# Four-layer graph network on one core: the variance and the negated mean of node phases 0 and 3 move from VectorE to GpSimd, and the gate of phase 3 becomes one product

## The chip, the cores and the metric

The kernel runs on one core of a Trainium2 chip. The metric is the device time of one execution in microseconds; 6471.27 us is the median of three runs of the kernel before.

## The reference

Four graph layers run one after the other on 50,000 nodes of 160 values (64 scalars, 32 vectors of three) and 25,000 edges. Each computes messages on the edges, adds them up by node, and ends with a residual and a normalisation:

```python
x = _layernorm(x + _L0_gnn_ref(x, ...), axis=-1)      # and so for L1, L2, L3
# _layernorm: (x - mean(x)) / sqrt(var(x) + 1e-5), over the 160 values of a node
# L0, node part:
angle = 0.1 * (ms @ W3) * node_attr * (1.0 / np.sqrt(MUL0 + MUL1))
cos, sin = (jnp.cos(angle), jnp.sin(angle))
return cos * sc + sin * conv                          # sc: a product of x with weights
# L3, node part: out_s, out_v = the sums from the edges plus a product of x with weights
fs = jax.nn.silu(out_s[:, :MUL0])
gate = jax.nn.sigmoid(out_s[:, MUL0:MUL0 + 32])
gv = gate[:, :, None] * out_v
return jnp.concatenate([fs, gv.reshape(N, -1)], axis=-1)
```

## The kernel before

Each layer has an edge phase, which adds messages into a table `agg` in device memory, and a node phase, which reads `x` and `agg` and writes the new `x`. The change touches two node phases: that of layer 0 (`node_phase_01`, called node phase 0) and that of layer 3 (`node_phase_3`).

A node phase goes over the nodes in 98 chunks of 512: 128 partitions with T = 4 nodes on each. Every engine has its own list of stages with a lag, `node_pipeline(engine, ((lag, stage), ...))`. At step m it runs its stages in the order of that list, each for chunk m - lag. The first 16 chunks and the last ones are written out, and the middle is a loop of eight chunks per turn. Engines meet by semaphores only; work buffers are double (`u = r % 2`), those of the transfers eightfold. GpSimd follows each wait with `fence`, an increment of a semaphore of its own. In the names of the trace the phase's tag is left out of this text: `rs` is `rs_n` there.

Node phase 0. SP loads `xr` and `ar`. TensorE transposes `xr` (L614, L617); ScalarE copies that to SBUF (`xta` L638, `xtb` L640); TensorE multiplies by the weights into `pk` (L625, L626). GpSimd makes the angle from `ar` (stage `angles`, `th` L720, `rn` L723, `th` L726 and L729), ScalarE its sine and cosine (stage `sines`, `ab` L646, `sn` L647, `cs` L649), and GpSimd the two factors (stage `factors`, `at` L737, `cf` L738). VectorE forms `y` = `pk` * `at` + `xr` (L680), then `ar` * `cf` + `y` (L686), the statistics of each node (`st` L693) and their mean and variance (`mv` L700), and in the stage `variance` `ve` = variance + 1e-5 (L706) and `nm` = -mean (L707). GpSimd's stage `deviation` raises `ve` to the power -1/2 (`rs` L751) and multiplies `nr` = `nm` * `rs` (L754). ScalarE's stage `normalise` writes `xn` = `rs` * `y` + `nr` (L657), which SP stores. The order of stages on an engine is

```python
node_pipeline(a, ((0, copy_turned), (4, normalise)) + (((1, sines),) if l == 0 else ()))
node_pipeline(v, ((3, skips), (3, sums), (3, moments), (3, join), (3, variance)))
node_pipeline(pool, ((1, factors), (3, deviation), (1, attribute)) + (((0, angles),) if l == 0 else ()))
```

Node phase 3 begins in the same way. VectorE's stage `layer` forms the scalars `ss` (L2154) and vectors `sv` (L2155) from `ar` and `pk`. ScalarE's stage `gates` makes `gt` = tanh(s/2) (L2130), and silu of the other scalars into `sg` (L2131). VectorE's stage `gate` multiplies (`gt` + 1) with `sv` into `sg`, one instruction for each of the four tiles (L2163); `total` adds `xr` into `y` (L2171); `moments` and `variance` make `st` (L2178), `mv` (L2186), `ve` (L2189) and `nm` (L2190). GpSimd has `deviation` alone (`rs` L2202, `nr` L2205); ScalarE's `normalise` is L2139. The order is

```python
node_pipeline(a, ((0, copy_turned), (3, normalise), (1, gates)))
node_pipeline(v, ((1, layer), (2, gate), (2, total), (2, moments), (2, variance)))
```

Of the kernel before, what the change touches and what calls it, by code (L numbers as in the profile page):

```python
# [23 lines left out]
P = 128  # L24
# [6 lines left out]
T = 4  # L31
# [494 lines left out]
def node_phase_01(nc, l, x, agg, xo, wt, width):  # L526

    with ExitStack() as ctx:
# [18 lines left out]
        cf = each(2, sb, "cf", [P, T])  # L547
        y = each(2, sb, "y", [P, T, D])
        st = sb("st", [P, T, 6])
        mv = sb("mv", [P, T, 2])  # L550
        ve = each(2, sb, "ve", [P, T])
        nm = each(2, sb, "nm", [P, T])
        rs = each(2, sb, "rs", [P, T])
        nr = each(2, sb, "nr", [P, T])
        xn = each(RN, sb, "xn", [P, T, XW])
# [107 lines left out]
        @block.vector  # L663
        def _(v):
            v.tensor_scalar(wt(f"na_{l}")[0:S0], wt(f"na_{l}")[0:S0], 1.0 / 8.0, None, ALU.mult).then_inc(folded, 1)
            v.tensor_scalar(wt(f"na_{l}")[S0:P], wt(f"na_{l}")[S0:P], 32.0 ** -0.5, None, ALU.mult).then_inc(folded, 1)
            v.tensor_scalar(wt(f"nb_{l}"), wt(f"nb_{l}"), 32.0 ** -0.5, None, ALU.mult).then_inc(folded, 1)
            if l == 0:
                v.memset(quarter[:], np.pi / 2).then_inc(folded, 1)
                v.tensor_scalar(turns[:], wt("attr"), 0.1 * 10.0 ** -0.5 * 96.0 ** -0.5 / (2 * np.pi), None, ALU.mult).then_inc(folded, 1)  # L670
                v.tensor_scalar(share[:], wt("attr"), 960.0 ** -0.5, None, ALU.mult).then_inc(folded, 1)

            def skips(c, r, k, parts):
                u = r % 2
                v.wait_ge(k_ps, c + 1)
                v.wait_ge(cf_ok, NCF * (c + 1))
                v.wait_ge(xn_ok, due(T * (c - 1)))
                for t in range(T):
                    by = at[u][:, t:t + 1] if l == 0 else xr[r][:, t, D:XW]
                    v.scalar_tensor_tensor(y[u][:, t, :], pk[u][:, t, 0:D], by, xr[r][:, t, 0:D], ALU.mult, ALU.add).then_inc(sk_ok, 1)  # L680

            def sums(c, r, k, parts):
                u = r % 2
                for t in range(T):
                    v.wait_ge(sk_ok, T * c + t + 1)
                    v.scalar_tensor_tensor(y[u][:, t, :], ar[r][:, t, 0:D], cf[u][:, t:t + 1], y[u][:, t, :], ALU.mult, ALU.add).then_inc(y_ok, 1)  # L686

            def moments(c, r, k, parts):
                u = r % 2
                v.wait_ge(st_ok, 8 * c)  # L690
                for t in range(T):
                    v.wait_ge(y_ok, T * c + t + 1)
                    v.bn_stats(st[:, t, :], y[u][:, t, :]).then_inc(st_ok, 1)  # L693

            def join(c, r, k, parts):
                v.wait_ge(ve_ok, 2 * c)
                v.wait_ge(st_ok, 8 * c + 4)
                fence(v)
                for t in range(T):
                    v.bn_aggr(mv[:, t, :], st[:, t, :]).then_inc(st_ok, 1)  # L700

            def variance(c, r, k, parts):
                u = r % 2
                v.wait_ge(st_ok, 8 * c + 8)
                v.wait_ge(rs_ok, due(2 * (c - 1)))
                v.tensor_scalar(ve[u][:], mv[:, :, 1], EPS, None, ALU.add).then_inc(ve_ok, 1)  # L706
                v.tensor_scalar(nm[u][:], mv[:, :, 0], -1.0, None, ALU.mult).then_inc(ve_ok, 1)  # L707

            node_pipeline(v, ((3, skips), (3, sums), (3, moments), (3, join), (3, variance)))

        @block.gpsimd
        def _(pool):
# [32 lines left out]
            def deviation(c, r, k, parts):  # L745
                u = r % 2
                pool.wait_ge(xn_ok, due(T * (c - 1)))
                fence(pool)
                pool.wait_ge(ve_ok, 2 * c + 2)
                fence(pool)  # L750
                pool.tensor_tensor(rs[u][:], ve[u][:], wt("mhalf"), ALU.pow).then_inc(rs_ok, 1)  # L751
                pool.wait_ge(rs_ok, 2 * c + 1)
                fence(pool)
                pool.tensor_tensor(nr[u][:], nm[u][:], rs[u][:], ALU.mult).then_inc(rs_ok, 1)  # L754

            pool.wait_ge(folded, 6)
            node_pipeline(pool, ((1, factors), (3, deviation), (1, attribute)) + (((0, angles),) if l == 0 else ()))
# [1268 lines left out]
def node_phase_3(nc, x, agg, out, wt):  # L2026

    with ExitStack() as ctx:  # L2028
# [8 lines left out]
        ss = each(2, sb, "ss", [P, T, 96])  # L2037
        sv = each(2, sb, "sv", [P, T, V3])
        gt = each(2, sb, "gt", [P, T, V1])
        sg = each(2, sb, "sg", [P, T, D])  # L2040
        y = each(2, sb, "y", [P, T, D])
        st = sb("st", [P, T, 6])
        mv = sb("mv", [P, T, 2])
        ve = each(2, sb, "ve", [P, T])
        nm = each(2, sb, "nm", [P, T])
        rs = each(2, sb, "rs", [P, T])
        nr = each(2, sb, "nr", [P, T])
        xn = each(RN, sb, "xn", [P, T, D])
# [66 lines left out]

        @block.scalar
        def _(a):
# [8 lines left out]
            def gates(c, r, k, parts):  # L2126
# [2 lines left out]
                a.wait_ge(y_ok, due(c - 1))  # L2129
                a.activation(gt[u][:], ss[u][:, :, S0:96], ACT.Tanh, scale=0.5).then_inc(act_ok, 1)  # L2130
                a.activation(sg[u][:, :, 0:S0], ss[u][:, :, 0:S0], ACT.Silu).then_inc(act_ok, 1)  # L2131

            def normalise(c, r, k, parts):

# [3 lines left out]
                for t in range(T):  # L2138
                    a.activation(xn[r][:, t, :], y[u][:, t, :], ACT.Identity, bias=nr[u][:, t:t + 1], scale=rs[u][:, t:t + 1]).then_inc(xn_ok, 1)  # L2139

            node_pipeline(a, ((0, copy_turned), (3, normalise), (1, gates)))

        @block.vector
        def _(v):
            v.tensor_scalar(wt("na_3")[:, 96:192], wt("na_3")[:, 96:192], 0.5, None, ALU.mult).then_inc(folded, 1)
            v.tensor_scalar(wt("nb_3"), wt("nb_3"), 0.5, None, ALU.mult).then_inc(folded, 1)

            def layer(c, r, k, parts):
# [30 lines left out]

            def variance(c, r, k, parts):  # L2180
                u = r % 2
                v.wait_ge(ve_ok, 2 * c)
                v.wait_ge(st_ok, 8 * c + 4)
                fence(v)
                for t in range(T):
                    v.bn_aggr(mv[:, t, :], st[:, t, :]).then_inc(st_ok, 1)  # L2186
                v.wait_ge(st_ok, 8 * c + 8)
                v.wait_ge(rs_ok, due(2 * (c - 1)))
                v.tensor_scalar(ve[u][:], mv[:, :, 1], EPS, None, ALU.add).then_inc(ve_ok, 1)  # L2189
                v.tensor_scalar(nm[u][:], mv[:, :, 0], -1.0, None, ALU.mult).then_inc(ve_ok, 1)  # L2190
# [4 lines left out]
        def _(pool):  # L2195
            def deviation(c, r, k, parts):
                u = r % 2
                pool.wait_ge(xn_ok, due(T * (c - 1)))
                fence(pool)
                pool.wait_ge(ve_ok, 2 * c + 2)  # L2200
                fence(pool)
                pool.tensor_tensor(rs[u][:], ve[u][:], wt("mhalf"), ALU.pow).then_inc(rs_ok, 1)  # L2202
                pool.wait_ge(rs_ok, 2 * c + 1)
                fence(pool)
                pool.tensor_tensor(nr[u][:], nm[u][:], rs[u][:], ALU.mult).then_inc(rs_ok, 1)  # L2205

            node_pipeline(pool, ((2, deviation),))

# [598 lines left out]
```

## Time and profile before

| | before |
|---|---|
| median of three runs | 6471.27 us (6468.07 to 6472.73) |
| the profiled execution | 6468.58 us |
| its span, first to last instruction | 6466.8 us |
| busy over the span: TensorE | 5101.9 us (79%) |
| VectorE | 4234.2 us (65%) |
| ScalarE | 2848.6 us (44%) |
| GpSimd | 4361.7 us (67%) |
| node phase 0, `rs` of the first to `rs` of the last chunk | 910.4 to 1338.3 us |
| node phase 3, the same | 6012.1 to 6460.2 us |

The shares are means over stages of very different kinds: edge phases fill most of the span. For the two node phases the timeline and the waits of their own stretch have to be read.

### The profile page before, as it was taken

How to read it: one execution, taken by the hardware profiler on the slowest of the kernel's cores; microseconds unless marked ns; L12 is line 12 of the kernel's file. 1: busy time of each engine (PE TensorE's matmuls, PEld its weight loads, DVE VectorE, ACT ScalarE, POOL GpSimd, SP SyncE). 2: the span in 40 equal slices, each digit the busy share in tenths (PEclk: the TensorE clock that was granted, in tenths of full speed). 3: DMA queues.
4: the chain of work that ended last, by engine and by line, in shares of the span. 5: the costliest groups of instructions: out<-in, count | busy, mean ns of one | idle time of the engine just before them, and what ended most of it. 6: DMA issues, size and time to landing. Idle time of an engine off the chain costs nothing. (4 is left out here: it accounts for less than half of the span.)

```text
span 6466.8 us, 123966 instructions
## 1 busy us (share of the span) xinstructions
PE 5101.9 (79%) x27989; PEld 3926.1 (61%) x28012; DVE 4234.2 (65%) x14730; ACT 2848.6 (44%) x6258; POOL 4361.7 (67%) x4641
## 2 busy tenths in 40 slices
PE   8889966679997886999655434338999989998776
PEld 6556656646666885767422134337888867776665
DVE  3566658854544786888677621216888878776788
ACT  5333347744443554444200000006777764443666
POOL 8688856658886877766277678875666657887222
PEclk9899989979998998999888766668999999999999
DMA  8566667736665663555311244443333325554665
GB/s 323 124 121 122 124 161 223 221 103 127 130 129 158 206 206 122 162 163 159 130 34 32 61 97 76 74 56 99 107 108 109 109 88 92 85 87 66 225 224 186
DMA packets 584565, 845.56 MB, mean 131 GB/s; under 512 B 216827, under 2 KB 334035, under 8 KB 579859
## 3 DMA queue, kind: packets, MB, share of 16 engines
q1 hardware_dynamic: 405587, 691.27, 33.5%
q0 software_dynamic: 178752, 151.88, 16.7%
q8 instruction: 68, 1.11, 0.1%
q14 instruction: 158, 1.29, 0.1%
HBM read 465.84 MB, written 375.78 MB: 130 GB/s over the span
## 5 line engine op out<-in xcount | busy, mean ns | idle before, releaser
L1143 POOL DMA_INDIRECT xg<-x,gidx x588 | 608.2, 1034 | 244.4 <-issue 181.1
L330 POOL DMA_INDIRECT agg<-summed,cidx x392 | 630.4, 1608 | 196.0 <-issue 111.5
L2020 PE MATMUL pc_a<-msg_a,same_a 128*128 128x168 f32 x980 | 258.1, 450 | 403.3 <-ACT summed_a L2007 346.4
L2020 PEld LDWEIGHTS pc_a<-msg_a,same_a 128*128 128x128 f32 x980 | 245.0, 305 | 416.9 <-issue 290.2
L403 DVE TENSOR_TENSOR pr<-pf,ws 128x512 f32<-128x512 f32 x196 | 135.6, 692 | 512.7 <-PE pf L490 395.6
L1154 POOL DMA_INDIRECT agg<-summed,cidx x196 | 317.5, 1620 | 78.2 <-issue 57.3
L1966 POOL DMA_INDIRECT agg<-summed_a,cidx_a x196 | 311.5, 1589 | 69.6 <-issue 58.5
L1317 ACT ACTIVATE ob<-po 128x416 f32<-128x416 f32 (+1 forms) x392 | 197.7, 504 | 354.0 <-PE po L1394 185.0
L1886 PE MATMUL pm_m<-arow_m,ones_m 128*128 128x512 bf16 x392 | 151.5, 477 | 227.6 <-DVE top_m L1833 225.3
L519 PEld LDWEIGHTS pc<-ob,same 128*128 128x128 f32 x1960 | 279.5, 194 | 83.4 <-issue 83.4
L2202 POOL TENSOR_TENSOR rs_n<-ve_n,wsb 128x4 f32<-128x4 f32 x98 | 98.7, 1007 | 338.0 <-DVE nm_n L2190 338.0
L2109 PE MATMUL pk_n<-wsb,xta_n 128*128 128x192 f32 x784 | 214.7, 356 | 121.2 <-ACT xtb_n L2124 121.2
L519 PE MATMUL pc<-ob,same 128*128 128x161 f32 x1960 | 303.4, 311 | 6.5 <-ACT summed L457 6.5
L1380 PE MATMUL ph<-esT,wsb 128*128 128x512 f32 x588 | 302.1, 595 | 2.3 <-DMA trow<-in_src_r 2.3
L625 PE MATMUL pk_n<-wsb,xta_n 128*128 128x160 f32 x784 | 190.2, 324 | 125.4 <-DVE y_n L680 112.6
L2007 ACT ACTIVATE summed_a<-pc_a 128x672 f32<-128x672 f32 x49 | 35.8, 731 | 561.1 <-DMA agg<-summed_a,cidx_a 559.0
L1252 DVE TENSOR_TENSOR pr<-pf,ws 128x512 f32<-128x512 f32 (+1 forms) x245 | 168.4, 687 | 150.8 <-PE pf L1368 83.9
L497 PE MATMUL ph<-hs,wsb 64*128 64x512 f32 x392 | 229.2, 666 | 47.9 <-ACT ws L444 45.5
L2556 POOL TENSOR_TENSOR rsa_n<-var_n,wsb 128x8 f32<-128x8 f32 x98 | 160.4, 1637 | 155.0 <-DVE var_n L2489 155.0
L1956 POOL DMA_INDIRECT big_a<-mx,tidx_a x196 | 197.1, 1006 | 92.0 <-issue 46.9
L1833 DVE TENSOR_REDUCE top_m<-pm_m 128x8 f32<-128x1024 f32 x196 | 238.7, 1221 | 24.6 <-PE pm_m L1888 24.1
L1303 ACT ACTIVATE ws<-ph 128x512 f32<-128x512 f32 x294 | 176.8, 601 | 171.2 <-PE ph L1380 166.9
(354 smaller groups left out, 17650.5 us busy)
## 6 DMA issues: line engine op xcount, KB each, us to landing
ar_n<-agg SPq DMA_DIRECT2D x194, 322.0 KB
agg<-zero SPq DMA_DIRECT2D x50, 768.0 KB
ar_n<-agg SPq DMA_DIRECT2D x97, 384.0 KB
agg<-zero SPq DMA_DIRECT2D x50, 672.0 KB
ar_n<-agg SPq DMA_DIRECT2D x97, 336.0 KB
agg<-zero_h SPq DMA_DIRECT2D x25, 1288.0 KB, 5.4
agg<-zero SPq DMA_DIRECT2D x50, 644.0 KB
x<-xn_n SPq DMA_DIRECT2D x97, 324.0 KB, 3.5
```

Source lines behind the costliest of these rows:

```text
L330: pool.indirect_dma_start(agg, bass.IndirectOffsetOnAxis(ap=cidx[r][:, t:t + 1], axis=0), summed[u][:, t, :], None, compute_op=ALU.add).th ...
L497: pe.matmul(ph[:], wt(f"w{g + 1}_{l}"), hs[NH - 1][:], start=True, stop=True).then_inc(w_ps, 1)
L519: last = pe.matmul(pc[:, t, 0:W], same[u][:, s, t * P:(t + 1) * P], ob[u][:, s, 32:32 + W], start=(s == t), stop=(s == T - 1))
L1143: pool.indirect_dma_start(xg[s][r][:, t, 0:XR], None, x, bass.IndirectOffsetOnAxis(ap=gidx[s][r][:, t:t + 1], axis=0)).then_inc(gathered[r ...
L1154: pool.indirect_dma_start(agg, bass.IndirectOffsetOnAxis(ap=cidx[r][:, t:t + 1], axis=0), summed[u][:, t, :], None, compute_op=ALU.add).th ...
L1317: a.activation(ob[u][:, t, :], po[:, t % 2, 0:TW], ACT.Copy).then_inc(ob_ok, 1)
L1380: pe.matmul(ph[:, (r + g) % 2 if l == 2 else 0], wt(f"w{g + 1}_{l}"), esT[r][:], start=True, stop=True).then_inc(w_ps, 1)
L1833: v.tensor_reduce(top[u][:, t, :], pm[HOME[t]][:], AX.X, ALU.max).then_inc(top_ok, 1)
L1956: pool.indirect_dma_start(big[r][:, t, :], None, mx, bass.IndirectOffsetOnAxis(ap=tidx[r][:, t:t + 1].bitcast(U32), axis=0)).then_inc(big_ ...
L1966: pool.indirect_dma_start(agg, bass.IndirectOffsetOnAxis(ap=cidx[r][:, t:t + 1], axis=0), summed[r % 2][:, t, :], None, compute_op=ALU.add ...
L2020: last = pe.matmul(pc[:, t, 0:W], same[u][:, s, t * P:(t + 1) * P], msg[u][:, s, :], start=(s == t), stop=(s == T - 1))
L2109: pe.matmul(pk[u][:, t, 0:192], xta[u][:, t * P:(t + 1) * P], wt("na_3"), start=True, stop=False)
```

## The change

In both phases `mv` gets two buffers, and `ve` and `nm` have one each. VectorE's chunk ends with `mv`. GpSimd's `deviation` waits for `mv` and for its own last `nr`, and issues `ve`, `nm`, `rs` and `nr`. In phase 3 ScalarE makes `ga` = `gt` + 1 besides (its bias is a column `one` that VectorE sets at the start), and VectorE's gate is one tensor_tensor over the four tiles.

```diff
 node phase 0
             def join(c, r, k, parts):
-                v.wait_ge(ve_ok, 2 * c)
+                v.wait_ge(rs_ok, due(2 * (c - 1)))
                 v.wait_ge(st_ok, 8 * c + 4)
                 fence(v)
                 for t in range(T):
-                    v.bn_aggr(mv[:, t, :], st[:, t, :]).then_inc(st_ok, 1)
-            def variance(c, r, k, parts):
-                u = r % 2
-                v.wait_ge(st_ok, 8 * c + 8)
-                v.wait_ge(rs_ok, due(2 * (c - 1)))
-                v.tensor_scalar(ve[u][:], mv[:, :, 1], EPS, None, ALU.add).then_inc(ve_ok, 1)
-                v.tensor_scalar(nm[u][:], mv[:, :, 0], -1.0, None, ALU.mult).then_inc(ve_ok, 1)
+                    v.bn_aggr(mv[u][:, t, :], st[:, t, :]).then_inc(st_ok, 1)
             def deviation(c, r, k, parts):
                 pool.wait_ge(xn_ok, due(T * (c - 1)))
                 fence(pool)
+                pool.wait_ge(st_ok, 8 * c + 8)
+                fence(pool)
+                pool.wait_ge(rs_ok, 2 * c)
+                fence(pool)
+                pool.tensor_scalar(ve[:], mv[u][:, :, 1], EPS, None, ALU.add).then_inc(ve_ok, 1)
+                pool.tensor_scalar(nm[:], mv[u][:, :, 0], -1.0, None, ALU.mult).then_inc(ve_ok, 1)
                 pool.wait_ge(ve_ok, 2 * c + 2)
                 fence(pool)
-                pool.tensor_tensor(rs[u][:], ve[u][:], wt("mhalf"), ALU.pow).then_inc(rs_ok, 1)
+                pool.tensor_tensor(rs[u][:], ve[:], wt("mhalf"), ALU.pow).then_inc(rs_ok, 1)
 node phase 3: the same, and
@@ scalar
                 a.activation(gt[u][:], ss[u][:, :, S0:96], ACT.Tanh, scale=0.5).then_inc(act_ok, 1)
                 a.activation(sg[u][:, :, 0:S0], ss[u][:, :, 0:S0], ACT.Silu).then_inc(act_ok, 1)
+                a.wait_ge(act_ok, 3 * c + 1)
+                a.activation(ga[u][:], gt[u][:], ACT.Identity, bias=one[:, 0:1], scale=1.0).then_inc(act_ok, 1)
@@ vector
+            v.memset(one[:], 1.0).then_inc(folded, 1)
             def gate(c, r, k, parts):
-                v.wait_ge(act_ok, 2 * c + 2)
+                v.wait_ge(act_ok, 3 * c + 3)
                 v.wait_ge(y_ok, due(c - 1))
-                for t in range(T):
-                    last = v.scalar_tensor_tensor(sg[u][:, t, S0:D].rearrange("p (u c) -> p u c", c=3), gt[u][:, t, :].unsqueeze(2).to_broadcast([P, V1, 3]), 1.0,
-                                                  sv[u][:, t, :].rearrange("p (u c) -> p u c", c=3), ALU.add, ALU.mult)
-                last.then_inc(sg_ok, 1)
+                v.tensor_tensor(sg[u][:, :, S0:D].rearrange("p t (u c) -> p t u c", c=3), sv[u][:].rearrange("p t (u c) -> p t u c", c=3),
+                                ga[u][:].unsqueeze(3).to_broadcast([P, T, V1, 3]), ALU.mult).then_inc(sg_ok, 1)
```

## Rows read from the trace of the kernel before

**Rows 1.** Records of `rs`, phases 0 and 3: count, ns min/median/max, first and last start.
```profile
L751 POOL TENSOR_TENSOR rs_n<-ve_n,wsb x98: 1006/1029/1190, 910.4 to 1338.3; 128x4 f32<-128x4 f32 x98
...
L2202 POOL TENSOR_TENSOR rs_n<-ve_n,wsb x98: 1006/1007/1041, 6012.1 to 6460.2; 128x4 f32<-128x4 f32 x98
```

**Rows 2.** Waits, 950 to 1300 us: us in total, times, longest.
```profile
ACT xn_n L657 <- POOL nr_n L754: 94.8, 79, 1.5
POOL at_n L737 <- ACT cs_n L649: 71.0, 79, 1.0
```

**Rows 3.** Timeline of phase 0: start us, busy us, engine, line, instruction.
```profile
1101.28 0.24 POOL L723 TENSOR_SCALAR rn_n<-th_n 128x4 f32<-128x4 f32 x1 [0.20 <-POOL th_n L720]
...
1101.70 0.20 POOL L726 TENSOR_TENSOR th_n<-th_n,rn_n 128x4 f32<-128x4 f32 x1 [0.18 <-POOL rn_n L723]
...
1102.29 0.16 DVE L707 TENSOR_SCALAR nm_n<-mv_n 128x4 f32<-128x4 f32 x1
...
1103.27 0.20 POOL L737 TENSOR_TENSOR at_n<-cs_n,wsb 128x4 f32<-128x4 f32 x1 [0.94 <-ACT cs_n L649]
1103.42 0.20 POOL L738 TENSOR_TENSOR cf_n<-sn_n,share_n 128x4 f32<-128x4 f32 x1
1103.60 1.03 POOL L751 TENSOR_TENSOR rs_n<-ve_n,wsb 128x4 f32<-128x4 f32 x1
...
1104.81 0.28 POOL L754 TENSOR_TENSOR nr_n<-nm_n,rs_n 128x4 f32<-128x4 f32 x1 [0.18 <-POOL rs_n L751]
...
1105.21 1.76 ACT L657 ACTIVATE xn_n<-y_n,nr_n,rs_n 128x160 f32<-128x160 f32 x4 [0.93 <-POOL nr_n L754]
...
1107.14 0.30 ACT L649 ACTIVATE cs_n<-ab_n,quarter_n 128x4 f32<-128x4 f32 x1
...
1107.71 0.20 POOL L737 TENSOR_TENSOR at_n<-cs_n,wsb 128x4 f32<-128x4 f32 x1 [0.93 <-ACT cs_n L649]
```

**Rows 4.** What ended GpSimd's idle time before `rs`, phase 0: us, times.
```profile
  DVE nm_n L707: 4.7, 2
```

**Rows 5.** Waits, 6050 to 6430 us.
```profile
POOL rs_n L2202 <- DVE nm_n L2190: 265.0, 82, 3.8
```

**Rows 6.** Busy us (x instructions): PE, PEld, DVE, ACT, POOL; clock, DMA share, GB/s.
```profile
6004.00:6008.00 4.00, 4.00 (x33) 4.00 (x32) 1.47 (x3) 1.59 (x4) 0.00 (x0) 0.96 0.85 325
...
6200.00:6250.00 50.00, 36.14 (x264) 33.54 (x263) 44.54 (x180) 34.39 (x87) 13.43 (x22) 1.00 0.66 226
```

**Rows 7.** Timeline of phase 3, one chunk of VectorE and what it depends on.
```profile
6207.32 0.29 ACT L2130 ACTIVATE gt_n<-ss_n 128x128 f32<-128x128 f32 x1
6207.52 0.40 ACT L2131 ACTIVATE sg_n<-ss_n 128x256 f32<-128x256 f32 x1
...
6208.72 0.55 DVE L2154 SCALAR_TENSOR_TENSOR ss_n<-ar_n,pk_n 128x384 f32<-128x384 f32 x1
...
6209.65 0.76 DVE L2163 SCALAR_TENSOR_TENSOR sg_n<-gt_n,sv_n 128x96 f32<-128x96 f32 x4
...
6210.54 0.82 DVE L2171 TENSOR_TENSOR y_n<-sg_n,xr_n 128x640 f32<-128x640 f32 x1
...
6211.01 0.36 PE L2110 MATMUL pk_n<-wsb,xtb_n 128*128 128x96 f32 x2
...
6212.65 0.38 DVE L2186 BATCH_NORM_AGGREGATE mv_n<-st_n 128x2 f32<-128x6 f32 x4 [0.16 <-DVE st_n L2178]
...
6213.06 0.17 DVE L2189 TENSOR_SCALAR ve_n<-mv_n 128x4 f32<-128x4 f32 x1
6213.14 0.16 DVE L2190 TENSOR_SCALAR nm_n<-mv_n 128x4 f32<-128x4 f32 x1
6213.32 0.55 DVE L2154 SCALAR_TENSOR_TENSOR ss_n<-ar_n,pk_n 128x384 f32<-128x384 f32 x1
```

**Rows 8.** Timeline of the edge phase before node phase 3, a product over 384 elements.
```profile
5911.98 0.56 DVE L1270 TENSOR_TENSOR m<-ob,yq 128x384 f32<-128x384 f32 x1
```

**Rows 9.** Records of `nr`, phase 0: ns min/median/max.
```profile
L754 POOL TENSOR_TENSOR nr_n<-nm_n,rs_n x98: 198/280/393, 911.8 to 1339.4; 128x4 f32<-128x4 f32 x98
```

More of the change, by code:

```diff
@@ L549, in node_phase_01 @@
         st = sb("st", [P, T, 6])
-        mv = sb("mv", [P, T, 2])
-        ve = each(2, sb, "ve", [P, T])
-        nm = each(2, sb, "nm", [P, T])
+        mv = each(2, sb, "mv", [P, T, 2])
+        ve = sb("ve", [P, T])
+        nm = sb("nm", [P, T])
         rs = each(2, sb, "rs", [P, T])
@@ L695, in join @@
             def join(c, r, k, parts):
-                v.wait_ge(ve_ok, 2 * c)
+                u = r % 2
+                v.wait_ge(rs_ok, due(2 * (c - 1)))
                 v.wait_ge(st_ok, 8 * c + 4)
@@ L699, in join @@
                 for t in range(T):
-                    v.bn_aggr(mv[:, t, :], st[:, t, :]).then_inc(st_ok, 1)
-            def variance(c, r, k, parts):
-                u = r % 2
-                v.wait_ge(st_ok, 8 * c + 8)
-                v.wait_ge(rs_ok, due(2 * (c - 1)))
-                v.tensor_scalar(ve[u][:], mv[:, :, 1], EPS, None, ALU.add).then_inc(ve_ok, 1)
-                v.tensor_scalar(nm[u][:], mv[:, :, 0], -1.0, None, ALU.mult).then_inc(ve_ok, 1)
-            node_pipeline(v, ((3, skips), (3, sums), (3, moments), (3, join), (3, variance)))
+                    v.bn_aggr(mv[u][:, t, :], st[:, t, :]).then_inc(st_ok, 1)
+            node_pipeline(v, ((3, skips), (3, sums), (3, moments), (3, join)))
         @block.gpsimd
@@ L748, in deviation @@
                 fence(pool)
+                pool.wait_ge(st_ok, 8 * c + 8)
[4 more added lines that the diff above has]
+                pool.tensor_scalar(nm[:], mv[u][:, :, 0], -1.0, None, ALU.mult).then_inc(ve_ok, 1)
                 pool.wait_ge(ve_ok, 2 * c + 2)
                 fence(pool)
-                pool.tensor_tensor(rs[u][:], ve[u][:], wt("mhalf"), ALU.pow).then_inc(rs_ok, 1)
+                pool.tensor_tensor(rs[u][:], ve[:], wt("mhalf"), ALU.pow).then_inc(rs_ok, 1)
                 pool.wait_ge(rs_ok, 2 * c + 1)
                 fence(pool)
-                pool.tensor_tensor(nr[u][:], nm[u][:], rs[u][:], ALU.mult).then_inc(rs_ok, 1)
+                pool.tensor_tensor(nr[u][:], nm[:], rs[u][:], ALU.mult).then_inc(rs_ok, 1)
             pool.wait_ge(folded, 6)
@@ L2039, in node_phase_3 @@
         gt = each(2, sb, "gt", [P, T, V1])
+        ga = each(2, sb, "ga", [P, T, V1])
+        one = sb("one", [P, 1])
         sg = each(2, sb, "sg", [P, T, D])
@@ L2042, in node_phase_3 @@
         st = sb("st", [P, T, 6])
-        mv = sb("mv", [P, T, 2])
-        ve = each(2, sb, "ve", [P, T])
-        nm = each(2, sb, "nm", [P, T])
+        mv = each(2, sb, "mv", [P, T, 2])
+        ve = sb("ve", [P, T])
+        nm = sb("nm", [P, T])
         rs = each(2, sb, "rs", [P, T])
@@ L2111, in skip @@
                 last.then_inc(k_ps, 1)
-            pe.wait_ge(folded, 2)
+            pe.wait_ge(folded, 3)
             node_pipeline(pe, ((0, turn_rows), (1, skip)))
@@ L2139, in normalise @@
                     a.activation(xn[r][:, t, :], y[u][:, t, :], ACT.Identity, bias=nr[u][:, t:t + 1], scale=rs[u][:, t:t + 1]).then_inc(xn_ok, 1)
+            a.wait_ge(folded, 3)
             node_pipeline(a, ((0, copy_turned), (3, normalise), (1, gates)))
@@ L2152, in layer @@
                 v.wait_ge(sg_ok, due(c - 1))
-                v.wait_ge(act_ok, due(2 * (c - 1)))
+                v.wait_ge(act_ok, due(3 * (c - 1)))
                 v.scalar_tensor_tensor(ss[u][:], ar[r][:, :, 0:96], 1.0 / 32.0, pk[u][:, :, 0:96], ALU.mult, ALU.add).then_inc(so_ok, 1)
@@ L2181, in variance @@
                 u = r % 2
-                v.wait_ge(ve_ok, 2 * c)
+                v.wait_ge(rs_ok, due(2 * (c - 1)))
                 v.wait_ge(st_ok, 8 * c + 4)
@@ L2185, in variance @@
                 for t in range(T):
[L2186 to L2190, printed above, removed]
+                    v.bn_aggr(mv[u][:, t, :], st[:, t, :]).then_inc(st_ok, 1)
             node_pipeline(v, ((1, layer), (2, gate), (2, total), (2, moments), (2, variance)))
@@ L2199, in deviation @@
                 fence(pool)
+                pool.wait_ge(st_ok, 8 * c + 8)
+                fence(pool)
+                pool.wait_ge(rs_ok, 2 * c)
+                fence(pool)
+                pool.tensor_scalar(ve[:], mv[u][:, :, 1], EPS, None, ALU.add).then_inc(ve_ok, 1)
+                pool.tensor_scalar(nm[:], mv[u][:, :, 0], -1.0, None, ALU.mult).then_inc(ve_ok, 1)
                 pool.wait_ge(ve_ok, 2 * c + 2)
                 fence(pool)
-                pool.tensor_tensor(rs[u][:], ve[u][:], wt("mhalf"), ALU.pow).then_inc(rs_ok, 1)
+                pool.tensor_tensor(rs[u][:], ve[:], wt("mhalf"), ALU.pow).then_inc(rs_ok, 1)
                 pool.wait_ge(rs_ok, 2 * c + 1)
                 fence(pool)
-                pool.tensor_tensor(nr[u][:], nm[u][:], rs[u][:], ALU.mult).then_inc(rs_ok, 1)
+                pool.tensor_tensor(nr[u][:], nm[:], rs[u][:], ALU.mult).then_inc(rs_ok, 1)
             node_pipeline(pool, ((2, deviation),))
```

## The prediction

> **What bounds the kernel now.** I first took the length of the two stages that the change touches. The instruction records of one GpSimd instruction give it [rows 1]: the power (`rs`) of node phase 0 starts 98 times between 910.4 and 1338.3, so a chunk takes 427.9 / 97 = 4.41 us; that of node phase 3 starts 98 times between 6012.1 and 6460.2, so a chunk takes 448.1 / 97 = 4.62 us. The two stages are about 14% of the span, and nothing else of the kernel is edited. Then I asked, for each stage, which wait ends last.
>
> Phase 0: the list of waits between 950 and 1300 (79 chunks) has two handovers that occur in every chunk [rows 2]: GpSimd's `at` waits for ScalarE's `cs` (71.0 / 79 = 0.90 us each time), and ScalarE's `xn` waits for GpSimd's `nr` (94.8 / 79 = 1.20 us). Two engines that wait for each other in every chunk form a closed ring. The timeline [rows 3] shows it link by link: `at` 1103.27, `cf` +0.15, `rs` +0.18, `nr` +1.21, `xn` +0.40, `cs` +1.93, next `at` at 1107.71, +0.57. The sum is 4.44 us, the chunk's length: the ring has no slack. VectorE is not in it. Its `nm` of the chunk was issued at 1102.29, over a microsecond before `rs`, and over the whole phase `rs` waited for `nm` just twice, 4.7 us in all [rows 4].
>
> Phase 3: here GpSimd does wait for VectorE, 265.0 / 82 = 3.2 us in each chunk [rows 5], and VectorE is busy 44.54 of 50 us [rows 6]. The timeline of VectorE [rows 7] is one unbroken row of instructions: `ss` 6208.72, `sg` 6209.65, `y` 6210.54, `mv` 6212.65, `ve` 6213.06, `nm` 6213.14, next `ss` 6213.32, 4.60 us, with gaps only of the length of a semaphore's round. VectorE's own order sets the pace.
>
> So the same edit (variance and negated mean moved from VectorE to GpSimd) takes work off the pacing engine in phase 3, and puts work on a pacing ring in phase 0.
>
> **Phase 0, step by step.** Removed from VectorE: `ve`, `nm` and a wait. That is worth nothing, as VectorE isn't in the ring. Added to GpSimd between `cf` and `rs`: a third wait, `ve`, `nm`, and `rs` must now wait for GpSimd's own `nm`. No row shows exactly this pair on GpSimd, so I bound it by its neighbours [rows 3]. From `ve` to `nm`, independent: 0.15 us (as `at` to `cf`, 128x4 operands), up to 0.19 if a tensor_scalar, 0.24 long against 0.20, holds its follower by the difference; I take 0.17. From `nm` to `rs`, dependent: `rn` to `th` is the same form, a tensor_scalar on 128x4 and a dependent instruction, 0.42 us (1101.28 to 1101.70); 0.39 at the least, if a single-operation tensor_scalar is a little shorter. The third wait: 0 to 0.15, I take 0.03. Sum 0.17 + 0.42 + 0.03 = 0.62 us per chunk, bounds 0.54 and 0.77. The new chunk is 4.41 + 0.62 = 5.03 us. Nothing hides it: GpSimd's idle 0.90 us lie before `at`, and the program's order keeps the pair behind `cf`. Queued behind the longer stretch are `nr`, `attribute` and `angles`, whose reader is ScalarE's `xn` and sines, both in the ring already. 98 x 0.62 = **+61 us** (53 to 75).
>
> **Phase 3, step by step.** The ending of VectorE's chunk: now `mv` to the next `ss` is 13.32 - 12.65 = 0.67 us [rows 7]. Without `ve`, `nm` and their waits `ss` follows `mv` directly: the four `mv` fill 0.38 us, and an instruction can be issued some 0.08 before the end of the one ahead (as `nm` after `ve`), so 0.30 at the least; at the most 0.48, `ve`'s place plus one issue step. The three waits of `layer` remain: I take 0.40, a saving of 0.27. The gate: now `sg` to `y` is 6210.54 - 6209.65 = 0.89 us. One product over 384 elements is 0.55 us (the same form with a broadcast operand [rows 8]), and then the waits of `total`: 0.03 to 0.15 more. I take 0.67, a saving of 0.22 (bounds 0.19 and 0.31). Together 0.49 us; VectorE's own chunk becomes 4.62 - 0.49 = 4.13 us.
>
> Here the Trainium skill could be set against the row: "VectorE: DVE Perf Modes", in the section on the TRN2 errata, gives an fp32 tensor_tensor (N + 151) / 0.96 ns. It fits the product of 384 (557 ns; the row has 0.55 us), but for four of 96 it would give 1.03 us, a saving of 0.47 instead of 0.22 and a total some 25 us lower. The row decides: the four run overlapped.
>
> ScalarE gains `ga` = tanh + 1, about 0.20 us of issue (as `gt`, of the same size, 6207.32 to 6207.52 [rows 7]). It lies behind `gt` and `silu`, and `silu` ends at 6207.92 while `sg` starts at 6209.65 [rows 7]: 1.7 us of cover. Two rings say what is late next. The first spans two chunks (gate, `y`, moments, GpSimd, `xn`, `ga`, gate): now 2 x 4.62 - 1.7 = 7.5 us, after it + 0.30 (the pair on GpSimd instead of VectorE) + 0.25 (`ga`) - 0.22 = 7.9, or 3.93 per chunk: under 4.13. The second spans three chunks (moments, GpSimd, `xn`, gates, copies, TensorE's skip, `ss`): TensorE ends `pk` at 6211.01 + 0.36 = 6211.37, and `ss` reads it at 6213.32, a slack of 1.95. So it is 3 x 4.60 - 1.95 = 11.85 now, after it + 0.30 + 0.20 - 0.22 = 12.1, or 4.04 per chunk. Also under 4.13, but near: VectorE paces still, and the ring caps the gain at about 0.58. I take 0.48 per chunk, for some stalls between the two: 98 x 0.48 = **-47 us** (-36 to -58). Loads aren't late: 226 GB/s become 253, and 325 were moved while the stage filled its buffers [rows 6]. The memset and the longer `folded` waits run while the first loads are under way, and cost nothing; if not, a few tenths once.
>
> **The sum.** +61 - 47 = +14 us. The profiled execution took 6468.6 us, 1.8 outside its span of 6466.8, and the median is 2.7 above it; neither is touched. 6471.3 + 14 = **6485 us**. Bounds: +53 - 58 = -5 and +75 - 36 = +39, so 6466 to 6510.
>
> **Rivals.** (A) *Phase 0 is paced by VectorE.* For it: VectorE has few gaps there, and loses the same 0.27 us. Then phase 0 falls by 26 us and phase 3 by 47: 6398 us. Against it: both handovers of the ring show in each of 79 chunks with about a microsecond each, where a pacing VectorE would leave one of them without a wait. It decides if these two waits are less than the 0.62 added. Chance 0.08. With it goes a milder form of the same place, 0.05: the pair costs only its issue step (0.30 in all), since GpSimd takes the dependent wait in its dispatch; then +29 - 47 = -18, 6453 us. The dependent steps of [rows 3] speak against that.
>
> (B) *GpSimd's small instructions are disturbed by VectorE.* `nr`, a 128x4 product, takes 198 to 393 ns, median 280 [rows 9]. If each of the new pair is drawn out by 0.1 us, phase 0 costs 20 us more: 6505 us; at 0.2 us, 6524. "GPSIMD Engine Reference" of the Trainium skill, section Key points, says that GpSimd contends with VectorE's instructions that have two SBUF inputs, of which phase 0 has four a chunk (`y` from `ar` and `y`); the spread of `nr` agrees. Chance 0.15.
>
> (C) *Phase 3 gains little,* as the waits of VectorE's loop stay at the new places and the three-chunk ring closes: 0.30 us a chunk instead of 0.48, -29 us, total 6503 us. For it: the ring is 0.1 from binding by my own sum. Chance 0.12.
>
> The forecast has 0.60. Under 0.2% (13 us) this kernel's measurement can't tell a change from none. Of the forecast's range (-5 to +39) a little over half lies above +13: slower 0.33, same 0.27; B and C add 0.22 to slower and 0.05 to same; A is faster (0.13). Slower 0.54, same 0.32, faster 0.14. A range of 6456 to 6512 leaves out A's strong form and B's upper end.
>
> **What the new profile would show.** Phase 0: `rs` starts 5.03 us apart, `cf` to `rs` at 0.8 instead of 0.18, and VectorE waits longer for `xn`. Phase 3: `rs` starts 4.14 apart; `mv` to `ss` 0.40, `sg` to `y` 0.67; GpSimd still waits for VectorE, about 2.3 us. Everything else unchanged. The prediction is wrong if the pair's steps on GpSimd are not near 0.17 and 0.42, if the handover waits of phase 0 vanish, or if TensorE's `pk` or ScalarE's `ga` ends VectorE's wait in phase 3.

## The result and the profile after

| | before | after |
|---|---|---|
| median | 6469.67 us (6466.33 to 6472.73, 4 runs) | 6514.28 us (6512.67 to 6517.31, 4 runs) |
| span of the profiled execution | 6466.8 us | 6512.5 us |
| VectorE busy | 4234.2 us | 4165.6 us |
| GpSimd busy | 4361.7 us | 4501.4 us |

The change made the kernel slower, by a ratio of 1.0070 (95% interval 1.0052 to 1.0087), 45 us. I had forecast 14 us slower, with 6456 to 6512 us as range; the time lies above it.

The instruction records of the profile after give the length of the two stages (name and line, ns min/median/max, first and last start). They answer to [rows 1]:

```profile
L751 POOL TENSOR_TENSOR rs_n<-ve_n,wsb x98: 1037/1196/1224, 909.8 to 1440.6; 128x4 f32<-128x4 f32 x98
...
L2208 POOL TENSOR_TENSOR rs_n<-ve_n,wsb x98: 1037/1038/1422, 6073.6 to 6505.9; 128x4 f32<-128x4 f32 x98
```

Phase 0 takes 530.8 us instead of 427.9, 5.47 us a chunk instead of 4.41: +103 us. Phase 3 takes 432.3 instead of 448.1, 4.46 us a chunk instead of 4.62: -16 us. That is +87, and the span grew by 45.7. The start of phase 3 shows that something else lies between: its first `rs` is 61.5 us later, not 103. The weight loads of the transposes of node phase 1, whose code is the same, tell where 39 of the 41 us between went. First the record of the kernel before, then that of the one after:

```profile
L855 PEld LDWEIGHTS pta_n<-wsb,xr_n x392: 138/141/231, 2034.2 to 2492.7; 128*128 128x128 f32 x196
```

```profile
L855 PEld LDWEIGHTS pta_n<-wsb,xr_n x392: 138/141/230, 2134.6 to 2554.2; 128*128 128x128 f32 x196
```

458.5 us became 419.6. Taken together +103 - 16 - 39 = +48, of which the span shows 45.7; the other 2 us are not attributed. What VectorE waited for at `y` of that phase (L910), before and after, over the whole phase (us, times); "issue" is time in which it waited for nothing that the profile shows:

```profile
DVE y_n L910 <- issue: 52.9, 10, 12.2
```

```profile
  PE pk_n L869: 27.8, 48
  issue: 12.3, 2
```

Beside a first wait of 12 us, which stays, nine waits of 4.1 to 5.1 us each are gone, some 39 us apart, as the turns of VectorE's loop are. They were in the rows of the kernel before all along; I had not looked at a stage in which no line was edited.

**Phase 0 after.** The waits between 950 and 1400 us (82 chunks), to be read against [rows 2]:

```profile
ACT xn_n L657 <- POOL nr_n L754: 178.2, 81, 2.5
...
DVE y_n L680 <- ACT xn_n L657: 133.8, 82, 1.9
POOL at_n L731 <- ACT cs_n L649: 70.3, 82, 1.0
```

Both handovers of the ring still show in each chunk: `at` waits 0.86 us for `cs` as before, `xn` waits 2.2 us for `nr` instead of 1.2, and VectorE now waits 1.6 us for `xn`. The timeline of GpSimd (start, busy us) gives the links, to be read against [rows 3]:

```profile
1193.82 0.20 POOL L731 TENSOR_TENSOR at_n<-cs_n,wsb 128x4 f32<-128x4 f32 x1 [0.84 <-ACT cs_n L649]
1193.97 0.20 POOL L732 TENSOR_TENSOR cf_n<-sn_n,share_n 128x4 f32<-128x4 f32 x1
1194.33 0.40 POOL L747 TENSOR_SCALAR ve_n<-mv_n 128x4 f32<-128x4 f32 x1 [0.15 <-issue]
1194.81 0.23 POOL L748 TENSOR_SCALAR nm_n<-mv_n 128x4 f32<-128x4 f32 x1
1195.23 1.20 POOL L751 TENSOR_TENSOR rs_n<-ve_n,wsb 128x4 f32<-128x4 f32 x1 [0.19 <-POOL nm_n L748]
1196.61 0.20 POOL L754 TENSOR_TENSOR nr_n<-nm_n,rs_n 128x4 f32<-128x4 f32 x1 [0.18 <-POOL rs_n L751]
```

`cf` to `rs` is 1.26 us here, where it was 0.18.

**Phase 3 after.** The waits between 6090 and 6460 us:

```profile
POOL ve_n L2204 <- ACT xn_n L2143: 134.4, 71, 2.0
...
ACT xn_n L2143 <- POOL nr_n L2211: 80.9, 84, 3.2
...
DVE ss_n L2160 <- PE pk_n L2112: 20.2, 38, 2.0
```

The last row is new: in about half of the chunks VectorE waits for TensorE, so it no longer sets the pace alone. The first row is a releaser taken from which event came last by the profile: in the timeline `mv` ends at 6254.43 and `ve` starts 0.35 later, so it is `mv` that it needed. The timeline, to be read against [rows 7]:

```profile
6251.94 0.83 DVE L2175 TENSOR_TENSOR y_n<-sg_n,xr_n 128x640 f32<-128x640 f32 x1
...
6252.27 0.55 POOL L2211 TENSOR_TENSOR nr_n<-nm_n,rs_n 128x4 f32<-128x4 f32 x1 [0.18 <-POOL rs_n L2208]
...
6254.05 0.38 DVE L2190 BATCH_NORM_AGGREGATE mv_n<-st_n 128x2 f32<-128x6 f32 x4 [0.16 <-DVE st_n L2182]
...
6254.53 0.55 DVE L2160 SCALAR_TENSOR_TENSOR ss_n<-ar_n,pk_n 128x384 f32<-128x384 f32 x1
...
6254.78 0.23 POOL L2204 TENSOR_SCALAR ve_n<-mv_n 128x4 f32<-128x4 f32 x1 [1.96 <-ACT xn_n L2143]
...
6258.26 0.38 DVE L2190 BATCH_NORM_AGGREGATE mv_n<-st_n 128x2 f32<-128x6 f32 x4 [0.16 <-DVE st_n L2182]
...
6258.50 0.36 PE L2112 MATMUL pk_n<-wsb,xtb_n 128*128 128x96 f32 x2
...
6258.99 0.55 DVE L2160 SCALAR_TENSOR_TENSOR ss_n<-ar_n,pk_n 128x384 f32<-128x384 f32 x1 [0.34 <-PE pk_n L2112]
```

`mv` to `ss` is 0.48 us in the first chunk and 0.73 in the second, where `ss` starts 0.13 us after TensorE's last `pk`. And `nr`, 0.20 us long when undisturbed, takes 0.55 and ends at 6252.82, just after VectorE's `y` (until 6252.77).

The start of the phase shows the ring over three chunks itself. A wait of 2.6 us for TensorE's `pk` in the first chunks comes back every third chunk (the rows of VectorE's `ss`, one in three):

```profile
6097.13 0.56 DVE L2160 SCALAR_TENSOR_TENSOR ss_n<-ar_n,pk_n 128x384 f32<-128x384 f32 x1 [1.52 <-PE pk_n L2112]
...
6110.90 0.56 DVE L2160 SCALAR_TENSOR_TENSOR ss_n<-ar_n,pk_n 128x384 f32<-128x384 f32 x1 [1.58 <-PE pk_n L2112]
...
6124.78 0.56 DVE L2160 SCALAR_TENSOR_TENSOR ss_n<-ar_n,pk_n 128x384 f32<-128x384 f32 x1 [1.69 <-PE pk_n L2112]
...
6138.97 0.55 DVE L2160 SCALAR_TENSOR_TENSOR ss_n<-ar_n,pk_n 128x384 f32<-128x384 f32 x1 [1.77 <-PE pk_n L2112]
```

In the kernel before, where the ring had 1.95 us to spare, `ss` waits for `pk` in the first two chunks and then once more at most; in best (below) one such wait of 1.6 us does not come back. How long such an echo lasts differs between runs of the same code of phase 3. Here it fills the first 24 chunks, in p3_only, where phase 3 takes 427 us, only some 12, and that is the 5 us between the two; in the middle of the phase a chunk takes 4.41 us in both.

### The profile page after: what moved, and what is told of

Same layout as the page of the kernel before. It is cut to its first block and busy times, and to the rows that moved or that the text cites. A ratio compares the mean times of both kernels' runs of the same rounds, so it can differ in the third digit from the quotient of the medians.

```text
span 6512.5 us, 124237 instructions
## 1 busy us (share of the span) xinstructions
PE 5154.2 (79%) x27989; PEld 3978.7 (61%) x28012; DVE 4165.6 (64%) x14045; ACT 2881.0 (44%) x6356; POOL 4501.4 (69%) x5033
## 5 line engine op out<-in xcount | busy, mean ns | idle before, releaser
L625 PE MATMUL pk_n<-wsb,xta_n 128*128 128x160 f32 x784 | 229.8, 382 | 163.7 <-DVE y_n L680 142.0
L657 ACT ACTIVATE xn_n<-y_n,nr_n,rs_n 128x160 f32<-128x160 f32 x392 | 171.9, 509 | 215.4 <-POOL nr_n L754 215.4
L497 PE MATMUL ph<-hs,wsb 64*128 64x512 f32 x392 | 230.1, 668 | 45.7 <-ACT ws L444 43.1
L625 PEld LDWEIGHTS pk_n<-wsb,xta_n 128*128 128x128 f32 x784 | 147.9, 235 | 185.3 <-DVE y_n L680 157.0
L1956 POOL DMA_INDIRECT big_a<-mx,tidx_a x196 | 196.9, 1005 | 92.1 <-issue 45.7
```

What stands on the lines that cost most here:

```text
L497: pe.matmul(ph[:], wt(f"w{g + 1}_{l}"), hs[NH - 1][:], start=True, stop=True).then_inc(w_ps, 1)
L625: pe.matmul(pk[u][:, t, 0:D], xta[u][:, t * P:(t + 1) * P], wt(f"na_{l}"), start=True, stop=False)
```

## The experiments

The stretches of each kernel, from the records of `nr` (phases 0 and 3: first to last start) and of the transposes of node phase 1, in us, with its ratio to the kernel before on the same chip:

| kernel | ratio (95% interval) | phase 0 | node phase 1 | phase 3 |
|---|---|---|---|---|
| before | 1 | 427.6 | 458.5 | 448.1 |
| after | 1.0070 (1.0052 to 1.0087) | 530.8 | 419.6 | 432.1 |
| p0_only | 1.0081 (1.0064 to 1.0097) | 530.7 | 420.5 | 446.1 |
| p3_only | 0.9960 (0.9946 to 0.9974) | 429.2 | 460.5 | 427.2 |
| before_pad | 0.9918 (0.9901 to 0.9934) | 428.0 | 419.6 | 447.8 |
| after_pad | 1.0121 (1.0104 to 1.0137) | 530.3 | 461.9 | 426.2 |
| p0_tt | 1.0051 (1.0031 to 1.0071) | 520.0 | 420.6 | 427.9 |
| p0_nowait | 1.0043 (1.0027 to 1.0059) | 517.8 | 418.8 | 428.2 |
| p0_first | 0.9910 (0.9894 to 0.9927) | 429.2 | 420.0 | 427.0 |
| p3_gate | 0.9969 (0.9959 to 0.9979) | 428.1 | 462.0 | 428.3 |
| p3_moments | 0.9964 (0.9952 to 0.9977) | 429.2 | 459.5 | 429.7 |
| gate_pad | 0.9913 (0.9897 to 0.9930) | 427.9 | 418.4 | 431.5 |
| gate_order_pad | 0.9908 (0.9891 to 0.9924) | 428.1 | 419.8 | 428.9 |
| best | 0.9871 (0.9854 to 0.9887) | 429.0 | 418.9 | 397.8 |

The four kernels from p0_only to after_pad ran on a chip on which the kernel before took 6703.29 us. The stretches of the table are as long there as elsewhere, so I compare those and the ratios, not the times.

### The halves apart, and the place of the code

p0_only has `node_phase_01` of the changed kernel and the rest of the one before; p3_only has `node_phase_3` alone.

> Node phase 0 with its edit, node phase 3 as before. The profiles before and after have rs of phase 0 103 us later at its end (427.9 to 531 us for 97 chunks), and node phase 1, whose code was not touched, shorter by 39 us. Theory: the pair on GpSimd costs 1.06 us a chunk, 103 us, and the shorter instruction list of VectorE moves the place of node phase 1's loop in that list, which ends its long waits named issue (52.9 us in 10 waits before, 12.3 us in 2 after). Then the time is 6470 + 103 - 39 = 6534 us, and node phase 1 takes about 420 us from its first to its last transpose instead of 458. Rival: the gain of node phase 1 comes from something else (phase 3's edit, or chance of one execution): then 6573 us.

> Node phase 3 with both of its edits, node phase 0 as before. Theory: phase 3 alone gains 0.163 us a chunk, 16 us, and nothing ahead of it changes: 6454 us, with node phase 1 at 458 us as before. Rival: if the 39 us of node phase 1 belong to phase 3's edit or to chance, 6415 us, or the 16 us vanish because they were chance too: 6470 us.

The two others add increments of a semaphore at the start of VectorE's list in node phase 0, 20 to the kernel before (before_pad) and 85 to the changed one (after_pad):

```diff
         @block.vector
         def _(v):
+            for _ in range(20):                  # after_pad: range(85)
+                v.sem_inc(turn, 1)
```

> The kernel before with 20 increments of a semaphore that nobody waits on, put at the start of VectorE's list in node phase 0. They compute nothing; they move the code of VectorE behind them by 20 instructions. Theory (place of the code): node phase 1's loop, 283 instructions of VectorE, begins at instruction 2298 of the list before, and at 2213 after the change, where the long waits are gone; at 2318 they go too, since the loop then lies in two blocks of 256 and not in three. 6470 - 39 = 6431 us. The Trainium skill, Runtime: NRT & Kernel Launch, section Instruction fetch mechanics, gives blocks of 256 instructions and two of them held at a time. Rival: node phase 1 got faster for another reason, such as when its data came: 6470 us.

> The changed kernel with 85 such increments at the start of VectorE's list in node phase 0, so that node phase 1's loop begins at instruction 2298 again, as in the kernel before. Theory (place of the code): the long waits of node phase 1 come back, 6514 + 39 = 6553 us, plus up to 2 us for the increments. Rival: node phase 1 stays at 420 us, 6515 us.

p0_only took 6757.85 us, 54.6 more than the kernel before, and node phase 1 has 420.5 us: the gain of node phase 1 comes with the edit of phase 0. p3_only took 25.0 less, of which its phase 3 shows 21, and node phase 1 stays at 460.5. The two padded kernels decide why. With 20 idle instructions more, the kernel before becomes faster by 53.3 us (0.9918) and its node phase 1 takes 419.6 us, 39 of the 53; the other 14 us are not attributed, and gate_pad, on another chip, gained 58 us, where its stretches show 40 and 17. With 85 more, the changed kernel becomes slower than p0_only and node phase 1 is back at 461.9. So it is the place of the loop in VectorE's list and nothing that the loop computes or gets. The traffic of the instruction queue over 360 to 400 us within node phase 1 (packets, MB, share) shows the mechanism, for before, after, before_pad and after_pad:

```profile
q14 instruction: 51, 0.42, 0.3%
```

```profile
q14 instruction: 5, 0.04, 0.0%
```

```profile
q14 instruction: 6, 0.05, 0.0%
```

```profile
q14 instruction: 51, 0.42, 0.3%
```

Where the loop is slow, code is loaded in every turn. VectorE's loop of node phase 1 has 283 instructions; it begins at number 2298 of the list in the two slow kernels, and at 2213 and 2318 in the two fast ones. The Trainium skill, "Runtime: NRT & Kernel Launch", section Instruction fetch mechanics, speaks of blocks of 256 instructions, two of which are held, and of a load where a branch leaves them. By that rule 2298 to 2580 lies in three blocks (they begin at 2048, 2304 and 2560), 2213 to 2495 and 2318 to 2600 in two each; the four traces agree. Other places, and the size of a block, were not tested.

### Phase 0: what the pair costs, and where it is free

```diff
 p0_tt, on the changed kernel (kc: columns of 1e-5 and of -1)
-                pool.tensor_scalar(ve[:], mv[u][:, :, 1], EPS, None, ALU.add).then_inc(ve_ok, 1)
-                pool.tensor_scalar(nm[:], mv[u][:, :, 0], -1.0, None, ALU.mult).then_inc(ve_ok, 1)
+                pool.tensor_tensor(ve[:], mv[u][:, :, 1], kc[:, 0:T], ALU.add).then_inc(ve_ok, 1)
+                pool.tensor_tensor(nm[:], mv[u][:, :, 0], kc[:, T:2 * T], ALU.mult).then_inc(ve_ok, 1)
 p0_nowait, on the changed kernel (ve and nm doubled)
-                pool.wait_ge(rs_ok, 2 * c)
-                fence(pool)
 p0_first, on the changed kernel (pair: the waits for mv and nr, ve and nm, taken out of deviation)
-            node_pipeline(pool, ((1, factors), (3, deviation), (1, attribute)) + (((0, angles),) if l == 0 else ()))
+            node_pipeline(pool, ((3, pair), (1, factors), (3, deviation), (1, attribute)) + (((0, angles),) if l == 0 else ()))
```

> The changed kernel, in whose node phase 0 GpSimd makes ve and nm by tensor_tensor with a constant tile (1e-5, -1) instead of tensor_scalar. In the profile after, ve to nm is 0.41 us in phase 0 and 0.31 in phase 3, where I had taken 0.17 from at to cf, two tensor_tensor 0.15 apart. Theory (form): a GpSimd tensor_scalar holds the next instruction until it is done, a tensor_tensor does not; then ve to nm falls to about 0.2 and a chunk of phase 0 from 5.47 to about 5.25 us (rs of phase 0: 510 us from the first to the last start instead of 531). Rival (operand): the strided reading of mv, or its sharing by both, holds it: ve to nm stays at 0.3 to 0.4, 531 us.

> The changed kernel, in whose node phase 0 ve and nm have two buffers each, so that GpSimd's third wait (for its own last nr) falls away. After, cf to ve is 0.40 us on the mean, where cf to rs was 0.22 before. Theory (waits): the third wait and its register work cost about 0.15 us between cf and ve, and a chunk falls from 5.47 to 5.32 us, rs 516 us from first to last. Rival (port): ve is held by VectorE's y from ar and y, with two operands in SBUF, that runs at this time; then cf to ve falls, but ve gets longer or nm later by as much, and the stretch stays at 531 us.

> The changed kernel, in whose node phase 0 ve and nm stand in a stage of their own ahead of factors, where GpSimd waits 0.9 us for ScalarE's cs in every chunk; the rest is unchanged. Theory (the ring of GpSimd and ScalarE paces phase 0, and the pair costs time because it lies in it): ve and nm fit into that wait, a chunk takes 4.45 to 4.6 us, rs 431 to 446 us from first to last instead of 531, and the time is 6514 - 92 = 6422 us on a chip where the kernel before takes 6470, or 0.7% below the kernel before. Rival (VectorE paces through mv): GpSimd then waits for mv ahead of factors, cf comes late for VectorE, and a chunk stays above 4.9 us.

The mean steps, from the timeline of some 75 to 85 chunks of each kernel from 950 us on, in us from start to start:

| | before | after | p0_tt | p0_nowait | p0_first |
|---|---|---|---|---|---|
| `cf` to `ve` (before, p0_first: to `rs`) | 0.22 | 0.40 | 0.38 | 0.30 | 0.22 |
| `ve` to `nm` | - | 0.41 | 0.25 | 0.32 | 0.31 |
| `nm` to `rs` | - | 0.43 | 0.50 | 0.43 | - |
| `rs` to `nr` | 1.24 | 1.35 | 1.38 | 1.37 | 1.24 |

p0_tt gained 11 us of the 20 expected: as products the two do lie closer, 0.25 us, so the form of the instruction is a part of it, but 0.07 came back behind `nm`. p0_nowait gained 13 of 15 us: the third wait costs 0.10 us itself, and `ve` to `nm` shrank as well, perhaps because `ve` moved in time against VectorE's `y`. Both are small. p0_first shows what mattered: the same pair with the same waits, ahead of `factors`, costs nothing: 429.2 us against 427.6. Its timeline of GpSimd:

```profile
1102.06 0.24 POOL L723 TENSOR_SCALAR th_n<-th_n 128x4 f32<-128x4 f32 x1 [0.20 <-POOL th_n L720]
1102.38 0.23 POOL L745 TENSOR_SCALAR ve_n<-mv_n 128x4 f32<-128x4 f32 x1
1102.69 0.23 POOL L746 TENSOR_SCALAR nm_n<-mv_n 128x4 f32<-128x4 f32 x1
1103.14 0.20 POOL L731 TENSOR_TENSOR at_n<-cs_n,wsb 128x4 f32<-128x4 f32 x1 [0.23 <-ACT cs_n L649]
```

`ve` and `nm` fill the time in which GpSimd waits for `cs`; 0.23 us of the 0.9 are left. The ring of GpSimd and ScalarE is shown by that as what paces phase 0: VectorE has as much work in both kernels, and the order on GpSimd alone takes 102 us away.

### Phase 3: each edit alone, and the ring opened

p3_gate and p3_moments are the kernel before with one of the two edits of phase 3. gate_pad is p3_gate with the 20 increments, gate_order_pad besides with ScalarE's stages in another order; best is p0_first with that order.

```diff
 gate_order_pad and best, node phase 3
-            node_pipeline(a, ((0, copy_turned), (3, normalise), (1, gates)))
+            node_pipeline(a, ((0, copy_turned), (1, gates), (3, normalise)))
```

> The kernel before with the gate of node phase 3 alone changed (ga on ScalarE, one product on VectorE); ve and nm stay on VectorE. Theory (VectorE paces phase 3, and the ring over three chunks has 1.95 us to spare): sg to y falls by 0.20 us, a chunk from 4.62 to 4.42, 20 us less in all, 0.3% faster than the kernel before. Rival: ga on ScalarE makes the ring close at once, and less than 10 us are gained.

> The kernel before with ve and nm of node phase 3 alone moved to GpSimd; the gate stays four instructions. The gate alone took a chunk of phase 3 from 4.62 to 4.42 us, and both edits together take 4.39 to 4.46. Theory (ring over three chunks: moments, GpSimd, xn, gates, copies, TensorE, ss): the move takes about 0.3 us from VectorE's own chunk and lengthens the ring by 0.9 to 1.1 us, of its 1.95 to spare; without ga in the ring it is just not closed, and a chunk takes 4.3 to 4.4 us: 21 to 31 us less than the kernel before. Rival (the move is worth nothing in itself, since VectorE stays late by the same amount for the port or the waits): 4.55 us or more, under 7 us gained.

> The changed kernel with the pair of node phase 0 ahead of factors, and in node phase 3 ScalarE's stages in the order copy_turned, gates, normalise instead of copy_turned, normalise, gates. That takes the three instructions of gates (0.8 us) out of the way from xn to the copies, so out of the ring over three chunks. Theory (this ring paces phase 3 after the change at 4.39 to 4.46 us): 0.8 / 3 = 0.27 us less, so VectorE's own order paces again, a chunk takes 4.15 to 4.25 us, 20 us less than the pair ahead of factors alone gave (0.9910 of the kernel before): about 0.988. Rival (GpSimd's slowed power and product or another ring of two chunks paces): no change in phase 3, 0.991.

> The kernel before with phase 3's gate as one product and the 20 increments that move node phase 1's loop; ve and nm stay on VectorE in both phases. Theory: the two gains that belong to the gate (20 us) and to the place of the code (39 us) are all that the best placing of the pair has reached (0.9910): this kernel takes 6470 - 59 = 6411 us, 0.991. Rival: the move of the pair has a worth of its own, and this kernel stays 10 us or more behind.

> As gate_pad, with ScalarE's stages of node phase 3 in the order copy_turned, gates, normalise. Theory: with ve and nm on VectorE its own order paces phase 3 (4.42 us a chunk), and a shorter ring gives nothing: the same as gate_pad. Against the kernel with the pair on GpSimd and the same order of stages it tells what the move is worth once the ring is open: 0.2 us a chunk, 20 us. Rival (the ring paces here too): 4.3 us or less.

The gate alone: 4.42 us a chunk, -20 us (in gate_pad, with the same phase 3, 4.45 and -17), with `sg` to `y` at 0.68 on the mean. The move alone: 4.43 us, -18 us by the stretch and 22 by the medians (6447.32 against 6469.1): at or just below the low end of what the ring's theory expected, and over the rival's 7. Both together: 4.39 to 4.46, hardly better than either; p0_first, with both, is at 0.9910 and gate_pad, with the gate alone, at 0.9913. The sum of two gains of 20 us is missing, and best finds it. With three instructions taken out of the way from `xn` to the copies, phase 3 takes 397.8 us, 4.10 a chunk where 4.15 to 4.25 were expected, and VectorE runs without a gap again:

```profile
6100.84 0.55 DVE L2163 SCALAR_TENSOR_TENSOR ss_n<-ar_n,pk_n 128x384 f32<-128x384 f32 x1
...
6104.57 0.38 DVE L2193 BATCH_NORM_AGGREGATE mv_n<-st_n 128x2 f32<-128x6 f32 x4 [0.16 <-DVE st_n L2185]
6104.97 0.56 DVE L2163 SCALAR_TENSOR_TENSOR ss_n<-ar_n,pk_n 128x384 f32<-128x384 f32 x1
```

The same order of stages gives nothing where `ve` and `nm` stay on VectorE (gate_order_pad, 428.9 against 431.5). With the ring open, the move of the pair is worth 428.9 less 397.8, 31 us, more than the 20 expected.

These stretches hold the start of the phase too. In the middle, from chunk 33 to 88, where each eight chunks take the same time, `ss` starts this far apart on the mean:

| | before | gate alone (p3_gate, gate_pad) | move alone (p3_moments) | both (after, p3_only) | both, other order (best) |
|---|---|---|---|---|---|
| us a chunk | 4.69 | 4.48, 4.50 | 4.37 | 4.41 | 4.13 |

So the move alone saves 0.32 us there. It is the larger of the two gains, and its stretch shows only 18 us since its start has the echo of the ring as well (4.91 us a chunk in the second eight chunks, 4.39 before). In these 56 chunks VectorE waits for `pk` 28 times with both edits, and never in any of the others: in the middle of the phase the ring over three chunks closes only when the pair is on GpSimd and `ga` on ScalarE, and adding the gate to the move then makes a chunk longer.

best is the fastest kernel of the study, 0.9871 of the one before.

## Why the prediction was wrong

**The structure held.** Phase 0 is paced by the ring of GpSimd and ScalarE with no slack, and nothing in it hides the pair (p0_first and after). Phase 3 was paced by VectorE, and the ring over three chunks caps the gain. Phase 0 loses and phase 3 gains, as forecast. Two of the signs that I had named for a wrong prediction came: `ve` to `nm` isn't near 0.17, and `pk` ends VectorE's wait in phase 3.

**Step 1, the size of the pair on GpSimd.** The term 0.17 + 0.42 + 0.03 = 0.62 us a chunk (53 to 75 us) measured 1.06 (103 us). Its parts: from `nm` to `rs` 0.43, right. From `ve` to `nm` 0.41 instead of 0.17 (upper bound 0.19); it was taken from two products, and a tensor_scalar followed by another isn't like these: 0.31 where nothing disturbs it (p0_first, and phase 3), and 0.41 in the place it had. The third wait 0.18 instead of 0.03 (p0_nowait: 0.10 of it is the wait). And `rs` to `nr` grew by 0.11, a term that the sum did not have. Together 0.24 + 0.01 + 0.15 + 0.11 = 0.51 above my term; 0.44 of it shows in the chunk, as `nr` to `xn` shrank by 0.08, from 0.34 to 0.26 on the mean.

**Rival B was partly right.** It had named this disturbance and priced it at 0.2 to 0.4 us a chunk. The rise of `rs` to `nr` and of `ve` to `nm` over its 0.31 makes 0.21 us, 21 us in all. In phase 3 it can be read directly: `nr` ends as VectorE's `y`, with both operands in SBUF, ends. The Trainium skill, "GPSIMD Engine Reference", section Key points, names contention with such instructions; these rows agree. All 98 `nr` of phase 3 after sort by it: the 65 that took over 0.3 us all overlap a `y` and end 0.06 us after it, and none of the other 33 overlaps one. That is a comparison within one run, not an experiment that took `y` away; p0_first, where `rs` to `nr` is 1.24 again, fits it.

**Step 2, phase 3.** The term -47 us (0.48 a chunk) measured -16 to -22 (0.16 to 0.22). VectorE's own chunk was sized right: 4.13 forecast, 4.10 over the stretch of best and 4.13 in its middle. What failed is the length of the ring over three chunks, which I made 12.1 us and which measures 3 x 4.46 = 13.4 over the whole stretch, 3 x 4.41 = 13.2 in its middle. Its terms by the mean steps of the timeline, before and after: `mv` to `rs` 0.85 and 1.46 us, so +0.61 where I had +0.30; `ga` +0.30 instead of 0.20; `rs` to `nr` 1.19 and 1.30, +0.12; `nr` to `xn` 0.31 and 0.51, +0.21 (of unrounded means); TensorE's first `pk` to `ss` 2.73, where I had counted 2.44 to the end of `pk`, +0.29; the gate -0.20. That is 11.85 + 1.33 = 13.2 us, or 4.39 a chunk, as measured in the runs between 426 and 428 us; the further 0.06 of the profile after is the longer echo at its start. The links of a closed path must add up to its three chunks, so this sum tells where the growth lies; that the ring paces is shown by the waits for `pk` and by best. I had the ring 0.09 us a chunk short of pacing, and it paced. Rival C, 0.30 us a chunk for just this reason, was nearer.

**Step 3, "everything else unchanged".** This failed by 39 us in the other direction. The removed instructions moved the code of VectorE, and node phase 1's loop fell into two blocks. It was luck that it ran against the other two errors and brought the time nearer to my forecast. Without it the change would have been some 84 us slower, as after_pad is: 82.0 us above the kernel before.

The forecast's +61 - 47 + 0 = +14 stands against +103 - 16 - 39 = +48 in the traces and +45 in the medians. So step 1 missed by 42 us, step 2 by 31, and step 3 took 39 of these 73 back.

## What to carry to other kernels

Before an instruction is moved to an engine that looks idle, find the rings of engines that wait for each other in every chunk, and put it where that engine waits, not behind the wait: the same two instructions cost 103 us behind `cf` and none ahead of `at`. When a step relieves the pacing engine, add up each ring with all its terms, as two gains of 20 us gave 16 to 22 together, and 50 (448 to 398 us) once a ring had been opened by the order of stages. Look for long waits without a releaser in every stage, edited or not: a loop's place in its engine's list was worth as much here as the whole result, and 20 idle instructions earned 0.8%.

## What the runs showed of the hardware

- Node phase 1, with a loop of 283 VectorE instructions, took 458 to 462 us with the loop at number 2298 of its list, and 418 to 421 us with it at 2213 and 2318, with 51 instruction packets against 5 or 6 in the time observed.
- On GpSimd a tensor_scalar on 128x4 is followed by an independent one after 0.31 us, a tensor_tensor by another after 0.15 us, though they last 0.23 and 0.20.
- GpSimd started `ve` 0.35 us after VectorE's `mv` had ended, with one more wait and two increments between (phase 3 after), and `rs` 0.18 us after `nm`, with one increment between (phase 3 before).
- GpSimd's 128x4 product took 194 to 791 ns (median 547) in phase 3 after, and the 65 of 98 that took over 300 ns all ended 0.06 us after a VectorE sum of two SBUF operands.
